# One normalisation instead of two, at both ends of a cross-attention over 8192 context rows

## The chip, the cores and the metric

The kernel runs on one core of a Trainium2 chip. The core has a matrix engine (PE, whose weight loads are listed apart as PEld), a vector engine (DVE), an activation engine (ACT), a general engine (POOL), a sync engine that issues transfers (SP), and 16 DMA engines. The metric is the device time of one execution in microseconds; lower is better.

## The reference, cut to what matters

A latent `x` of 512 rows by 512 columns passes through five blocks. Each block reads a row-normalised `x` and adds its output to `x`. The change touches the entry of the third-last block (cross-attention over 8192 context rows) and the entry of the second-last one (channel attention), because each of these two normalises its input once more:

```python
def _layernorm(x, axis=-1, eps=1e-05):
    m = jnp.mean(x, axis=axis, keepdims=True)
    v = jnp.var(x, axis=axis, keepdims=True)
    return (x - m) / jnp.sqrt(v + eps)
...
    # _L1_xattn_ref(x, latents, ...), EPS = 1e-05
    ln = layernorm(latents, gl, bl)      # (x - mu) * rsqrt(var + EPS) * g + b
    q = ln @ Wq
    kv_input = jnp.concatenate([xn, ln], axis=-2)
    kv = kv_input @ Wkv
...
    # _L1_attn_ref(x, gamma, ...), EPS = 1e-12
    xn = _l2norm(x) * dim ** 0.5 * gamma # t / max(sqrt(sum(t * t)), EPS)
    qkv = xn @ w_qkv
...
    x = x + _L1_xattn_ref(ctx_1024, _layernorm(x, axis=-1), L1_xattn_Wq, ...)
    x = x + _L1_attn_ref(_layernorm(x, axis=-1), L1_attn_gamma, ...)
    x = x + _L1_ffn_ref(_layernorm(x, axis=-1), ...)
```

So the rows are layer-normalised twice in a row ahead of the cross-attention, and layer-normalised and then scaled to unit length ahead of the channel attention.

## The kernel before

The 512 rows of `x` stay on the core in `x_res` as four tiles of 128 rows (index `tt`, `TT` = 4). Every engine has one program, written out by hand, and the engines meet through semaphores. There is no scheduler: the order of the calls is the order of the work.

A hand-over between two blocks is a short stretch of its own. The matrix engine ends the block with one output tile per `tt`. DVE adds the tile to `x_res` (line 1700 at the entry of the cross-attention, line 1869 at its exit, line 1953 at the exit of the channel attention). `ln_measure` (lines 1441 and 1442) takes mean and variance of the rows with two DVE instructions. POOL makes the scale from the variance with two small instructions: it adds the epsilon and raises to the power -0.5 (lines 813 and 814; at the cross-attention's entry lines 909 and 910 in `twice_scale`). `ln_row` (line 1447) writes the normalised tile `xn` on DVE. PE transposes the four tiles, and ACT and DVE split them into a high and a low half (`xT_hi`, `xT_lo`), with which the next block's products start. DVE handles tile `tt - 1` while POOL works on tile `tt`.

**Entry of the cross-attention.** After the first `ln_row` of a tile, DVE measures `xn` itself, POOL makes a second scale, and a second `ln_row` rescales `xn` in place. `TWICE` numbers the eight `ln_row` calls. PE transposes (line 2262) wait on the second one. Behind the last of them DVE inverts and splits the context's deviations (`sd`, lines 1711 to 1715), makes the low half of the query weights (`wq_lo`, line 1728), applies gain and bias (`affine`, line 1723) and splits the result (line 1743). PE meanwhile transposes `sd` (line 2267) and makes `bv` (line 2272: 32 products with one moving column each, whose stationary side is the raw weight `wkv_raw`); after them in its program come the query products (lines 2083 to 2085). The weights come by transfers that SP issues once the last output tile of the block before is complete:

```python
sp.wait_ge(s3_out, TT)
sp.dma_start(wq_raw[:], ...)     # line 662
sp.dma_start(wkv_raw[:], ...)    # line 663
```

ACT makes `wq_hi` from `wq_raw` (line 1195).

**Exit of the cross-attention.** After `ln_row`, ACT squares `xn` with a running sum (`sum_sq`, line 1300), POOL bounds the sum from below and raises it to -0.5 (lines 951 and 953), and DVE scales `xn` in place (`unit_row`, line 1864). PE transposes (line 2092) wait on that; then ACT and DVE split (lines 1304 and 1879), and the products of the channel attention start (line 2083).

Of the kernel before, what the change touches and what calls it, by code (L numbers as in the profile page):

```python
# [7 lines left out]
ACT = mybir.ActivationFunctionType  # L8
ALU = mybir.AluOpType
AX = mybir.AxisListType  # L10

P = 128
T = 512
D = 512
TT, DT = T // P, D // P
BANK = 512
LN_EPS = 1e-5
# [97 lines left out]

SQUARED = (1, 2, 4, 6)
UNIT_ROWS = [5 * TT + n for n in (3, 5, 7, 8)]
TWICE = ((0, 1, 3, 5), (2, 4, 6, 7))

# [79 lines left out]
def build(nc, a, out):  # L199
    ctx = ExitStack()  # L200
    with ctx:
# [186 lines left out]
        t5 = s5("t5", [P, XPAIRS])  # L388
        sum_sq = s5("sum_sq", [P, TT])

# [136 lines left out]
        def retire(engine, *counts):  # L527
# [13 lines left out]
        p5_mm, n5_sum, s5_sim, a5_T, o5_mm, s5_out = again("pe", "mm", "sum", "sim", "aT", "o", "out")  # L541
        w5_hi, x5_sq, p5_hi, p5_sq, t5_exp, s5_exp, a5_hi, o5_hi = again(
            "act", "w_hi", "x_sq", "p_hi", "p_sq", "t_exp", "exp", "a_hi", "o_hi")
        n5_sqrt = Signal(sem("n5_sqrt"))
        w5_lo, g5_ready, p5_lo, n5_read, s5_shift, s5_bd, a5_lo, o5_lo, s5_x = again(
            "dve", "w_lo", "gamma", "p_lo", "read", "shift", "bd", "a_lo", "o_lo", "x")
        x5_rn, n5_rs, bd_zero = again("pool", "rn", "rs", "zero")
        retire("pe", (p5_mm, UNITS), (n5_sum, 2 * XCB), (s5_sim, 2), (a5_T, 2), (o5_mm, XPAIRS), (s5_out, TT),
# [5 lines left out]
               (peak_neg, PAIRS), (shift_split, PAIRS), (o_inv, 1), (o_norm, PAIRS))  # L554
        retire("pool", (x5_rn, 2 * TT), (n5_rs, 1), (bd_zero, 1))
        retire("dma", (w4_q_loaded, 16), (w4_kv_loaded, 16), (w4_out_loaded, 16), (cT_loaded0, 16 * (KCHUNKS - 1) // 2), (cT_loaded1, 16 * (KCHUNKS - 1) // 2),
# [242 lines left out]
        def _(pool):  # L799
# [105 lines left out]

            def twice_scale(n, tt):

                pool.wait_ge(ln_stats, 3 * TT + n + 1)
                link(pool, nc.gpsimd.tensor_scalar(ln_ve[:, tt:tt + 1], ln_mv[:, tt, 1:2], LN_EPS, None, ALU.add))
                nc.gpsimd.tensor_tensor(ln_rstd[:, tt:tt + 1], ln_ve[:, tt:tt + 1], neg_half[:, tt:tt + 1], ALU.pow).then_inc(ln_scaled, 1)  # L910

            for n, tt in enumerate((0, 1, 0, 2, 1, 3, 2, 3)):
                twice_scale(n, tt)
            nc.gpsimd.memset(scale_rows[:].bitcast(F32), 0.0).then_inc(s4_init.sem, 1)
# [32 lines left out]
            def unit_scale(tt):  # L947

                one = slice(tt, tt + 1)
                pool.wait_ge(*x5_sq(tt + 1))  # L950
                nc.gpsimd.tensor_scalar(sum_sq[:, one], sum_sq[:, one], TINY, None, ALU.max).then_inc(x5_rn.sem, 1)
                pool.wait_ge(*x5_rn(2 * tt + 1))
                nc.gpsimd.tensor_tensor(sum_sq[:, one], sum_sq[:, one], neg_half[:, one], ALU.pow).then_inc(x5_rn.sem, 1)

            ln_scale(5, 0)
            for tt in range(1, TT):
                ln_scale(5, tt)
                unit_scale(tt - 1)
            unit_scale(TT - 1)
            nc.gpsimd.memset(attn_bd[:], 0.0).then_inc(bd_zero.sem, 1)  # L960
# [3 lines left out]

            ln_scales(6)
            link(pool, nc.gpsimd.memset(before[:], 1.0))
# [17 lines left out]
        def _(act_e):  # L984
# [312 lines left out]

            for tt in range(TT):
                act_e.wait_ge(xn_ready, 5 * TT + SQUARED[tt])
                nc.scalar.activation(squares[:, tt], xn[:, tt], ACT.Square, accum_out=sum_sq[:, tt:tt + 1]).then_inc(x5_sq.sem, 1)  # L1300
            act_e.wait_ge(*g5_ready(1))
# [3 lines left out]
            for c in range(3 * XCB):  # L1305
                for j in range(4):
# [13 lines left out]
                    if c < 2 * XCB:  # L1320
                        if j == 0:
                            if c == 0:
                                act_e.wait_ge(*x5_sq(TT))
                            else:
                                act_e.wait_ge(*n5_sum(c))
                        nc.scalar.activation(squares[:, j], ps[:, n % 4], ACT.Square).then_inc(p5_sq.sem, 1)
                        nc.scalar.activation(qk_hi[:, c // XCB, j, c % XCB * CB:(c % XCB + 1) * CB], ps[:, n % 4],
                                             ACT.Copy).then_inc(p5_hi.sem, 1)
                    else:
                        nc.scalar.activation(vT_hi[:, n - QK_UNITS], ps[:, n % 4], ACT.Copy).then_inc(p5_hi.sem, 1)  # L1330
# [45 lines left out]
            for tt in range(TT):  # L1376
                act_e.wait_ge(xn_ready, 7 * TT + tt + 1)
                if tt:
                    act_e.wait_ge(*x6_sq(tt))
                nc.scalar.activation(s_gate[:], xn[:, tt], ACT.Square, accum_out=r6[:, tt:tt + 1]).then_inc(x6_sq.sem, 1)  # L1380
# [55 lines left out]
        def _(dve):  # L1436
# [259 lines left out]
            level_out(HB // HQ - 1)  # L1696
            for tt in range(TT + 2):
                if tt < TT:
                    dve.wait_ge(s3_out, tt + 1)
                    nc.vector.scalar_tensor_tensor(x_res[:, tt], ps[:, tt], t_back[:, 1, tt:tt + 1], x_res[:, tt],  # L1700
                                                   ALU.mult, ALU.add).then_inc(s3_x, 1)
                    dve.wait_ge(s3_x, tt + 1)
                    ln_measure(tt, x_res)
                if 1 <= tt <= TT:
                    ln_row(3 * TT + TWICE[0][tt - 1], tt - 1, x_res)
                    dve.wait_ge(xn_ready, 3 * TT + TWICE[0][tt - 1] + 1)
                    ln_measure(tt - 1, xn)
                if tt >= 2:
                    ln_row(3 * TT + TWICE[1][tt - 2], tt - 2, xn)
            dve.wait_ge(rs_ready, 1)  # L1710
# [150 lines left out]

            def unit_row(tt):
                dve.wait_ge(*x5_rn(2 * tt + 2))
                nc.vector.tensor_scalar(xn[:, tt], xn[:, tt], sum_sq[:, tt:tt + 1], None, ALU.mult).then_inc(xn_ready, 1)

            for tt in range(TT + 2):
                if tt < TT:
                    dve.wait_ge(*s4_out(tt + 1))
                    nc.vector.tensor_tensor(x_res[:, tt], ps[:, 4 + tt], x_res[:, tt], ALU.add).then_inc(s4_x.sem, 1)
                    dve.wait_ge(*s4_x(tt + 1))  # L1870
                    ln_measure(tt, x_res)
                if 1 <= tt <= TT:
                    ln_row(5 * TT + tt - 1, tt - 1, x_res)
                if tt >= 2:
                    unit_row(tt - 2)
            dve.wait_ge(*g5_ready(1))
# [78 lines left out]

            ln_rows(6, add_fifth)
            ln_low(3)
# [121 lines left out]
        def _(pe):  # L2079
# [179 lines left out]
            for j in range(KT):  # L2259
                pe.wait_ge(xn_ready, 3 * TT + TWICE[1][j] + 1)  # L2260
                for dt in range(DT):
# [232 lines left out]

            ln_transpose(UNIT_ROWS)

# [80 lines left out]

            ln_transpose(range(7 * TT + 1, 8 * TT + 1))
            pe.wait_ge(xT_lo_ready, 4 * DT)
# [171 lines left out]
```

## Time and profile before

| | |
|---|---|
| time, three runs | 2758.85, 2763.52, 2764.38 us, median 2763.52 |
| profiled execution | 2763.65 us, its span 2761.9 us |
| PE busy | 2532.4 us, 92% of the span |
| DVE busy | 1852.6 us, 67% |
| ACT busy | 1109.3 us, 40% |
| POOL busy | 570.1 us, 21% |
| mean granted clock of PE | 0.957 |

Busy time is what an engine spent in instructions; a share of the span says nothing about which engine is waited for in a given stretch. In the rows further down, a timeline row is: start, duration, engine, line and operation, tile written and tiles read, shapes and count, and in brackets how long the engine had been idle and what released it.

### The profile page before, as it was taken

The page shows a single profiled execution, that of the slowest core. Times are in us where ns is not written, and L with a number is a line of the kernel's source. Part 1 is how long each engine was busy: PE and PEld are TensorE (multiplying, and loading weights), DVE is VectorE, ACT ScalarE, POOL GpSimd, SP SyncE. Part 2 cuts the span into 40 slices and gives each one's busy share as a digit, 9 for nine tenths or more (in the row PEclk, how much of TensorE's full clock was granted, in tenths as well). Part 3 has the DMA queues.
Part 4 walks back from the last instruction along what each step waited for, and adds up shares of the span by engine and source line. Part 5 has one row for each costly group of instructions (what it writes and reads, how often), then busy time and mean ns, then how long its engine had stood idle before and what let it go on. Part 6 is the DMA issues. An engine that isn't in the chain of part 4 may idle for free.

```text
span 2761.9 us, 33609 instructions
## 1 busy us (share of the span) xinstructions
PE 2532.4 (92%) x11618; PEld 1677.2 (61%) x11618; DVE 1852.6 (67%) x2025; ACT 1109.3 (40%) x1343; POOL 570.1 (21%) x413
## 2 busy tenths in 40 slices
PE   6999988967765799999999999999899799999999
PEld 5778867732222677777764444444477577777776
DVE  5877843189988677778886666666534666666665
ACT  2334322144435322222235555555332455554553
POOL 4555542078850211111110000000000100000000
PEclk9999989989986799999999999999989899999999
DMA  7677745710010233433322223222100366666663
GB/s 275 227 240 262 261 115 162 272 62 16 15 69 10 104 135 133 164 140 141 149 92 107 92 93 130 97 91 91 61 31 31 132 235 221 223 221 222 228 228 133
DMA packets 105455, 394.47 MB, mean 143 GB/s; under 512 B 22842, under 2 KB 23046, under 8 KB 73108
## 3 DMA queue, kind: packets, MB, share of 16 engines
q1 hardware_dynamic: 77380, 326.61, 32.3%
q10 hardware_dynamic: 27984, 66.66, 7.0%
q8 instruction: 56, 0.92, 0.1%
q14 instruction: 35, 0.29, 0.0%
HBM read 303.93 MB, written 89.30 MB: 142 GB/s over the span
## 4 chain that ended last, share of the span: by engine, by line
PE 77%; DVE 10%; DMA 6%; issue 3%; POOL 2%; ACT 1%; ACTq 0%; DVEq 0%; SPq 0%; POOLq 0%
PE ps L2083 17%; PE ps L2084 16%; PE ps L2085 16%; PE ps L2430 10%; PE ps L2439 9%; DVE ps L1595 4%; DMA w_halves<-unit_lo 4%; PE ps L2342 3%; DVE drive L1595 1%; PE ps L2673 1%; PE ps L2236 1%; POOL drive L878 1%; DMA sh_raw<-in_s_parts 1%; DMA wT_lo<-w_halves 1%; DVE ln_st L1441 1%
## 5 line engine op out<-in xcount | busy, mean ns | idle before, releaser
L1835 DVE TENSOR_TENSOR sums<-sums,pT 128x1024 f32<-128x1024 f32 x272 | 333.2, 1225 | 195.7 <-ACT pT L1270 181.4
L1778 DVE SCALAR_TENSOR_TENSOR peak<-ps,rs_all,peak 128x1024 f32<-128x1024 f32 x272 | 335.5, 1277 | 95.1 <-PE ps L2342 94.7
L1270 ACT ACTIVATE pT<-ps,rs_all 128x1024 f32<-128x1024 f32 x272 | 288.3, 1112 | 231.9 <-DVE sums L1835 128.5
L2439 PE MATMUL ps<-pT,values 128*64 128x512 f32 x1088 | 263.4, 605 | 0.0
L2188 PE MATMUL ps<-read,ident 128*128 128x512 f32 x256 | 144.7, 679 | 72.6 <-POOL read L891 37.2
L878 POOL TENSOR_TENSOR drive<-x_conv,bc_all 128x1024 f32<-128x1024 f32 x64 | 150.5, 2374 | 100.9 <-PE ps L2085 100.9
L926 POOL TENSOR_TENSOR cT_lo<-cT_raw,cT_hi 128x512 fp32r<-128x512 f32 x64 | 82.7, 1294 | 347.6 <-ACT cT_hi L1222 347.6
L1970 DVE TENSOR_TENSOR rgu_lo<-rgu_raw,rgu_hi 128x2048 fp32r<-128x2048 f32 x64 | 143.9, 2288 | 5.1 <-ACT rgu_hi L1353 5.1
L2188 PEld LDWEIGHTS ps<-read,ident 128*128 128x128 f32 x256 | 45.6, 205 | 166.7 <-DVE read L1601 77.4
L2439 PEld LDWEIGHTS ps<-pT,values 128*64 128x64 f32 x1088 | 66.0, 136 | 126.4 <-issue 126.4
L1136 ACT ACTIVATE ps<-delta,a_neg 128x512 f32<-128x512 f32 (+1 forms) x128 | 88.5, 692 | 126.8 <-DVE read L1601 113.4
L813 POOL TENSOR_SCALAR ln_ve<-ln_mv 128x1 f32<-128x1 f32 x20 | 7.3, 364 | 627.6 <-DVE ln_mv L1442 627.4
L826 POOL TENSOR_TENSOR ctx_lo<-ctx_raw,ctx_hi 128x512 fp32r<-128x512 f32 x64 | 106.2, 1660 | 129.4 <-DVE ctx_hi L1476 129.4
L1210 ACT ACTIVATE key_hi<-ps 128x512 fp32r<-128x512 f32 x68 | 40.7, 599 | 203.8 <-PE ps L2085 203.8
L2430 PE MATMUL ps<-q_lo,key_hi 64*128 64x512 f32 x544 | 121.2, 442 | 0.0
L2430 PEld LDWEIGHTS ps<-q_lo,key_hi 64*128 64x128 f32 x544 | 50.8, 183 | 115.5 <-ACT pT L1270 106.3
L1964 DVE TENSOR_TENSOR sh_lo<-sh_raw,sh_hi 128x1536 fp32r<-128x1536 f32 x32 | 56.3, 1758 | 93.2 <-ACT sh_hi L1348 93.2
L1353 ACT ACTIVATE rgu_hi<-rgu_raw 128x2048 fp32r<-128x2048 f32 x64 | 118.8, 1907 | 0.0
L1595 DVE TENSOR_TENSOR_SCAN ps<-ps,drive 128x512 f32<-128x512 f32 x96 | 116.9, 1218 | 2.2 <-POOL drive L878 2.2
L2083 PE MATMUL ps<-xT_hi,ctxT_lo 128*128 128x512 f32 x256 | 102.8, 402 | 14.4 <-DVE ctxT_lo L1478 14.4
L2083 PE MATMUL ps<-cT_hi,wp_lo 128*128 128x512 f32 x256 | 107.8, 421 | 8.9 <-POOL cT_lo L926 8.9
L1215 ACT ACTIVATE values<-ps,rs_all 128x512 f32<-128x512 f32 x68 | 46.9, 690 | 163.5 <-PE ps L2085 163.5
(436 smaller groups left out, 6362.3 us busy)
## 6 DMA issues: line engine op xcount, KB each, us to landing
rgu_raw<-in_r_gate_up SPq DMA_DIRECT2D x64, 1024.0 KB, 4.8
rd_raw<-in_r_down SPq DMA_DIRECT2D x32, 1024.0 KB, 4.8
sh_raw<-in_s_parts SPq DMA_DIRECT2D x32, 768.0 KB, 4.3
key_rows<-key_hi SPq DMA_DIRECT2D x17, 1024.0 KB, 3.9
key_rows<-key_lo SPq DMA_DIRECT2D x17, 1024.0 KB, 5.9
value_rows<-values SPq DMA_DIRECT2D x17, 1024.0 KB, 8.7
ctxT_raw<-in_ctx_T SPq DMA_DIRECT2D x16, 1024.0 KB, 6.7
ctx_raw<-in_ctx SPq DMA_DIRECT2D x16, 1024.0 KB, 8.6
```

The source lines that it names most:

```text
L878: nc.gpsimd.tensor_tensor(drive[:, g % SCAN_AHEAD], x_conv[:, ib].unsqueeze(1).to_broadcast([P, SG, T]), b_all[:, g * SG:(g + 1) * SG], AL ...
L1270: nc.scalar.activation(pT[:, kt], ps[:, kt % 2 * 2:kt % 2 * 2 + 2], ACT.Exp, scale=rs_all[:, bass.ds(c * KT + kt, 1)]).then_inc(s4_exp.sem, 1)
L1595: nc.vector.tensor_tensor_scan(source if far(g, e) else ps[:, DECAY_BANK + e], ps[:, DECAY_BANK + e], source, 0.0, ALU.mult, ALU.add).then ...
L1778: nc.vector.scalar_tensor_tensor(peak[:, p], ps[:, b:b + 2], rs_all[:, bass.ds(c * KT + kt, 1)], peak[:, p], ALU.mult, ALU.max).then_inc(s ...
L1835: nc.vector.tensor_tensor(sums[:, p], sums[:, p], pT[:, kt], ALU.add).then_inc(s4_sum.sem, 1)
L1970: nc.vector.tensor_tensor(rgu_lo[:, j % 2, i], rgu_raw[:, j % 2, i], rgu_hi[:, j % 2, i].bitcast(F32), ALU.subtract).then_inc(rgu_low.sem, 1)
L2083: nc.tensor.matmul(o, l_lo, r_hi, start=start, stop=False)
L2084: nc.tensor.matmul(o, l_hi, r_lo, start=False, stop=False)
L2085: return nc.tensor.matmul(o, l_hi, r_hi, start=False, stop=stop)
L2188: done = nc.tensor.matmul(ps[:, b], ident[:], read[:, g % SCAN_AHEAD, e], start=g == 0 and e == 0, stop=g == SGS - 1 and e == SG - 1)
L2430: done = nc.tensor.matmul(ps[:, kt % 2 * 2 + e], key[rows], query[rows], start=m == 0, stop=m == len(parts) - 1)
L2439: done = nc.tensor.matmul(ps[e * DK:(e + 1) * DK, 4 + p], values[:, s, kt, h * DK:(h + 1) * DK], pT[:, kt, e], start=start and kt == 0, st ...
```

## The change

Both double normalisations become one. With v the variance of a row and e the epsilon, the second layer normalisation sees variance v / (v + e), so both scales together are (v(1 + e) + e²)^-0.5. At the exit the sum of squares of the normalised row is D v / (v + e), so both scales together are (D v)^-0.5, bounded as before. In each case POOL computes the product directly from the first variance, in the same two instructions with other constants, and `ln_row` runs once for a tile. The second measuring, the four ACT squares, the tile `sum_sq`, the second POOL pair and the second DVE scaling are gone. The numbers for which `xn_ready`, `ln_stats` and `ln_scaled` are waited follow.

```diff
-SQUARED = (1, 2, 4, 6)
-UNIT_ROWS = [5 * TT + n for n in (3, 5, 7, 8)]
-TWICE = ((0, 1, 3, 5), (2, 4, 6, 7))
...
-            def twice_scale(n, tt):
-
-                pool.wait_ge(ln_stats, 3 * TT + n + 1)
-                link(pool, nc.gpsimd.tensor_scalar(ln_ve[:, tt:tt + 1], ln_mv[:, tt, 1:2], LN_EPS, None, ALU.add))
+            def twice_scale(tt):
+
+                pool.wait_ge(ln_stats, 3 * TT + tt + 1)
+                link(pool, nc.gpsimd.tensor_scalar(ln_ve[:, tt:tt + 1], ln_mv[:, tt, 1:2], 1.0 + LN_EPS, LN_EPS * LN_EPS, ALU.mult, ALU.add))
...
-            for n, tt in enumerate((0, 1, 0, 2, 1, 3, 2, 3)):
-                twice_scale(n, tt)
+            for tt in range(TT):
+                twice_scale(tt)
...
-                one = slice(tt, tt + 1)
-                pool.wait_ge(*x5_sq(tt + 1))
-                nc.gpsimd.tensor_scalar(sum_sq[:, one], sum_sq[:, one], TINY, None, ALU.max).then_inc(x5_rn.sem, 1)
-                pool.wait_ge(*x5_rn(2 * tt + 1))
-                nc.gpsimd.tensor_tensor(sum_sq[:, one], sum_sq[:, one], neg_half[:, one], ALU.pow).then_inc(x5_rn.sem, 1)
-
-            ln_scale(5, 0)
-            for tt in range(1, TT):
-                ln_scale(5, tt)
-                unit_scale(tt - 1)
-            unit_scale(TT - 1)
+                pool.wait_ge(ln_stats, 4 * TT + tt + 1)
+                link(pool, nc.gpsimd.tensor_scalar(ln_ve[:, tt:tt + 1], ln_mv[:, tt, 1:2], float(D), TINY * LN_EPS, ALU.mult, ALU.max))
+                nc.gpsimd.tensor_tensor(ln_rstd[:, tt:tt + 1], ln_ve[:, tt:tt + 1], neg_half[:, tt:tt + 1], ALU.pow).then_inc(ln_scaled, 1)
+
+            for tt in range(TT):
+                unit_scale(tt)
...
-            for tt in range(TT):
-                act_e.wait_ge(xn_ready, 5 * TT + SQUARED[tt])
-                nc.scalar.activation(squares[:, tt], xn[:, tt], ACT.Square, accum_out=sum_sq[:, tt:tt + 1]).then_inc(x5_sq.sem, 1)
...
-            for tt in range(TT + 2):
+            for tt in range(TT + 1):
...
-                if 1 <= tt <= TT:
-                    ln_row(3 * TT + TWICE[0][tt - 1], tt - 1, x_res)
-                    dve.wait_ge(xn_ready, 3 * TT + TWICE[0][tt - 1] + 1)
-                    ln_measure(tt - 1, xn)
-                if tt >= 2:
-                    ln_row(3 * TT + TWICE[1][tt - 2], tt - 2, xn)
+                if tt:
+                    ln_row(3 * TT + tt - 1, tt - 1, x_res)
...
-                if 1 <= tt <= TT:
-                    ln_row(5 * TT + tt - 1, tt - 1, x_res)
-                if tt >= 2:
-                    unit_row(tt - 2)
+                if tt:
+                    ln_row(4 * TT + tt - 1, tt - 1, x_res)
...
-                pe.wait_ge(xn_ready, 3 * TT + TWICE[1][j] + 1)
+                pe.wait_ge(xn_ready, 3 * TT + j + 1)
...
-            ln_transpose(UNIT_ROWS)
+            ln_transpose(range(4 * TT + 1, 5 * TT + 1))
```

This is DVE's program at the entry of the cross-attention before the change, the end of the eight normalisations and what stands behind them (`xn` are the normalised rows, `ln_mv` mean and variance, `sd` the context's deviations):

```order
L1441 BN_STATS ln_st<-xn 128x6
L1442 BN_AGGR ln_mv<-ln_st 128x2
L1447 TENSOR_SCALAR xn<-xn,ln_mv,ln_rstd 128x512
L1447 TENSOR_SCALAR xn<-x_res,ln_mv,ln_rstd 128x512
L1441 BN_STATS ln_st<-xn 128x6
L1442 BN_AGGR ln_mv<-ln_st 128x2
L1447 TENSOR_SCALAR xn<-xn,ln_mv,ln_rstd 128x512 x2
L1711 RECIPROCAL sd<-rs_all 128x68
```

The same place after the change, from the last addition to `x_res` on:

```order
L1686 SCALAR_TENSOR_TENSOR x_res<-ps,t_back,x_res 128x512
L1427 BN_STATS ln_st<-x_res 128x6
L1428 BN_AGGR ln_mv<-ln_st 128x2
L1433 TENSOR_SCALAR xn<-x_res,ln_mv,ln_rstd 128x512 x2
L1693 RECIPROCAL sd<-rs_all 128x68
L1694 CAST sd_parts<-sd 128x68
```

The twelve DVE instructions that read `xn` are gone, and the inversion of `sd` stands directly behind the fourth normalisation; nothing else moved.

This is DVE's program at the exit of the cross-attention before the change (`sum_sq` is the sum of squares of a row, `gamma` the gain):

```order
L1869 TENSOR_TENSOR x_res<-ps,x_res 128x512
L1441 BN_STATS ln_st<-x_res 128x6
L1442 BN_AGGR ln_mv<-ln_st 128x2
L1447 TENSOR_SCALAR xn<-x_res,ln_mv,ln_rstd 128x512
L1864 TENSOR_SCALAR xn<-xn,sum_sq 128x512
L1447 TENSOR_SCALAR xn<-x_res,ln_mv,ln_rstd 128x512
L1864 TENSOR_SCALAR xn<-xn,sum_sq 128x512 x2
L1879 SCALAR_TENSOR_TENSOR xT_lo<-ps,gamma_52,xT_hi 128x512 x4
```

And after it:

```order
L1847 TENSOR_TENSOR x_res<-ps,x_res 128x512
L1427 BN_STATS ln_st<-x_res 128x6
L1428 BN_AGGR ln_mv<-ln_st 128x2
L1433 TENSOR_SCALAR xn<-x_res,ln_mv,ln_rstd 128x512 x2
L1855 SCALAR_TENSOR_TENSOR xT_lo<-ps,gamma_52,xT_hi 128x512 x4
```

The four scalings by `sum_sq` are gone from DVE, and each addition to `x_res` follows the normalisation directly.

Besides, the semaphores are dealt out again, since two are no longer needed. In the loop over six experts of the last block, DVE's program has 5 register instructions more in a turn, which compute the values that it waits for; the programs of PE and SP have the same rows as before.

## Rows read from the trace of the kernel before

**Rows 1.** Windows: busy time by stretch, clock and DMA share.

```profile
core 0: us, PE busy (x) PEld busy (x) DVE busy (x) ACT busy (x) POOL busy (x), PEclk, DMA share, GB/s
891.00:915.00 24.00, 14.49 (x64) 11.11 (x62) 22.23 (x41) 6.34 (x7) 8.58 (x17) 0.61 0.59 223
968.00:1975.00 1007.00, 1003.92 (x5408) 590.73 (x5408) 714.39 (x626) 407.19 (x467) 84.36 (x66) 1.00 0.29 114
1996.00:2011.00 15.00, 6.75 (x26) 4.52 (x25) 11.51 (x22) 4.98 (x12) 8.22 (x17) 0.70 0.10 38
```

**Rows 2.** Timeline of DVE, entry of the cross-attention.

```profile
891.35 0.75 DVE L1700 SCALAR_TENSOR_TENSOR x_res<-ps,t_back,x_res 128x512 f32<-128x512 f32 x1 [2.41 <-PE ps L2246]
892.97 0.72 DVE L1700 SCALAR_TENSOR_TENSOR x_res<-ps,t_back,x_res 128x512 f32<-128x512 f32 x1
...
905.41 1.14 DVE L1447 TENSOR_SCALAR xn<-xn,ln_mv,ln_rstd 128x512 f32<-128x512 f32 x1 [0.77 <-POOL ln_rstd L910]
...
907.63 2.29 DVE L1728 TENSOR_TENSOR wq_lo<-wq_raw,wq_hi 128x2048 fp32r<-128x2048 f32 x1
912.72 2.48 DVE L1743 TENSOR_TENSOR xT_lo<-affine,xT_hi 128x512 fp32r<-128x512 f32 x4
```

**Rows 3.** Timeline of SP, ACT and PE, the same place.

```profile
894.37 0.51 SPq L663 DMA_DIRECT2D wkv_raw<-in_L_xattn_Wkv  x1
899.40 1.91 ACT L1195 ACTIVATE wq_hi<-wq_raw 128x2048 fp32r<-128x2048 f32 x1 [11.18 <-DMA wq_raw<-in_L_xattn_Wq]
907.80 6.95 PEld L2272 LDWEIGHTS ps<-b_ctx,wkv_raw 128*128 128x128 f32 x32
915.26 0.79 PE L2083 MATMUL ps<-xT_hi,wq_lo 128*128 128x512 f32 x1 [0.42 <-DVE xT_lo L1743]
```

**Rows 4.** Tile wkv_raw: its one transfer from issue to landing.

```profile
DMA to landing us min/median/max: 10.2/10.2/10.2
```

**Rows 5.** Timeline of DVE, exit of the channel attention.

```profile
2140.99 0.69 DVE L1953 TENSOR_TENSOR x_res<-ps,x_res 128x512 f32<-128x512 f32 x1 [7.52 <-PE ps L2085]
...
2142.55 0.66 DVE L1953 TENSOR_TENSOR x_res<-ps,x_res 128x512 f32<-128x512 f32 x1
...
2149.30 0.55 DVE L1447 TENSOR_SCALAR xn<-x_res,ln_mv,ln_rstd 128x512 f32<-128x512 f32 x1 [0.77 <-POOL ln_rstd L814]
```

**Rows 6.** Timeline, exit of the cross-attention.

```profile
1995.88 0.69 DVE L1869 TENSOR_TENSOR x_res<-ps,x_res 128x512 f32<-128x512 f32 x1 [3.33 <-PE ps L2085]
...
2004.83 0.55 DVE L1447 TENSOR_SCALAR xn<-x_res,ln_mv,ln_rstd 128x512 f32<-128x512 f32 x1 [0.46 <-POOL ln_rstd L814]
...
2007.13 1.14 DVE L1864 TENSOR_SCALAR xn<-xn,sum_sq 128x512 f32<-128x512 f32 x1 [0.81 <-POOL sum_sq L953]
...
2010.60 0.76 PE L2083 MATMUL ps<-w_hi,xT_lo 128*128 128x512 f32 x1 [1.15 <-DVE xT_lo L1879]
```

**Rows 7.** Windows of 1 us where the clock of PE rises.

```profile
920.00:921.00 1.00, 1.00 (x5) 0.78 (x5) 0.00 (x0) 0.47 (x1) 1.00 (x2) 0.98 0.00 0
...
2015.00:2016.00 1.00, 1.00 (x4) 0.85 (x3) 0.00 (x0) 0.00 (x1) 0.00 (x0) 0.64 0.00 0
```

**Rows 8.** Chain that ended last: products after a restart, at either clock.

```profile
1985.22 0.76 PE ps L2083
...
1988.11 0.43 PE ps L2083
1989.00 0.24 PE ps L2083
```

**Rows 9.** Timeline of DVE, two steps of the expert loop, two written out.

```profile
2320.64 0.68 DVE L2059 TENSOR_TENSOR r_act<-ps,r_gate 80x512 f32<-80x512 f32 x1
2337.43 0.68 DVE L2059 TENSOR_TENSOR r_act<-ps,r_gate 80x512 f32<-80x512 f32 x1
...
2655.97 0.68 DVE L2059 TENSOR_TENSOR r_act<-ps,r_gate 80x512 f32<-80x512 f32 x1
2672.68 0.68 DVE L2059 TENSOR_TENSOR r_act<-ps,r_gate 80x512 f32<-80x512 f32 x1
```

More of the change, by code:

```diff
@@ L388, in build @@
         t5 = s5("t5", [P, XPAIRS])
-        sum_sq = s5("sum_sq", [P, TT])
         s6 = Map(nc, base, 229344)
@@ L541, in build @@
         p5_mm, n5_sum, s5_sim, a5_T, o5_mm, s5_out = again("pe", "mm", "sum", "sim", "aT", "o", "out")
-        w5_hi, x5_sq, p5_hi, p5_sq, t5_exp, s5_exp, a5_hi, o5_hi = again(
-            "act", "w_hi", "x_sq", "p_hi", "p_sq", "t_exp", "exp", "a_hi", "o_hi")
+        w5_hi, p5_hi, p5_sq, t5_exp, s5_exp, a5_hi, o5_hi = again(
+            "act", "w_hi", "p_hi", "p_sq", "t_exp", "exp", "a_hi", "o_hi")
         n5_sqrt = Signal(sem("n5_sqrt"))
@@ L546, in build @@
             "dve", "w_lo", "gamma", "p_lo", "read", "shift", "bd", "a_lo", "o_lo", "x")
-        x5_rn, n5_rs, bd_zero = again("pool", "rn", "rs", "zero")
+        n5_rs, bd_zero = again("pool", "rs", "zero")
         retire("pe", (p5_mm, UNITS), (n5_sum, 2 * XCB), (s5_sim, 2), (a5_T, 2), (o5_mm, XPAIRS), (s5_out, TT),
@@ L554, in build @@
                (peak_neg, PAIRS), (shift_split, PAIRS), (o_inv, 1), (o_norm, PAIRS))
-        retire("pool", (x5_rn, 2 * TT), (n5_rs, 1), (bd_zero, 1))
+        retire("pool", (n5_rs, 1), (bd_zero, 1))
         retire("dma", (w4_q_loaded, 16), (w4_kv_loaded, 16), (w4_out_loaded, 16), (cT_loaded0, 16 * (KCHUNKS - 1) // 2), (cT_loaded1, 16 * (KCHUNKS - 1) // 2),
@@ L962, in _ @@
             nc.gpsimd.tensor_tensor(rq[:], rq[:], neg_half[:, 0:XPAIRS], ALU.pow).then_inc(n5_rs.sem, 1)
-            ln_scales(6)
+            ln_scales(5)
             link(pool, nc.gpsimd.memset(before[:], 1.0))
@@ L1321, in _ @@
                         if j == 0:
-                            if c == 0:
-                                act_e.wait_ge(*x5_sq(TT))
-                            else:
+                            if c:
                                 act_e.wait_ge(*n5_sum(c))
@@ L1376, in _ @@
             for tt in range(TT):
-                act_e.wait_ge(xn_ready, 7 * TT + tt + 1)
+                act_e.wait_ge(xn_ready, 5 * TT + tt + 1)
                 if tt:
@@ L1860, in _ @@
             qkv_lo(1)
[L1862 to L1866, printed above, removed]
+            for tt in range(TT + 1):
                 if tt < TT:
@@ L1954, in add_fifth @@
                 dve.wait_ge(*s5_x(tt + 1))
-            ln_rows(6, add_fifth)
+            ln_rows(5, add_fifth)
             ln_low(3)
@@ L2575, in _ @@
                     weigh_rows(p + 4)
-            ln_transpose(range(7 * TT + 1, 8 * TT + 1))
+            ln_transpose(range(5 * TT + 1, 6 * TT + 1))
             pe.wait_ge(xT_lo_ready, 4 * DT)
```

## The prediction

> **What bounds the kernel now.** I read the busy time by stretch first, since the change touches two short stretches only. In the long middle of the cross-attention PE is busy in 1003.9 of 1007 us: that part is PE's own, and a change ahead of it can only shift it. The two hand-overs are the opposite. Around the entry PE has work for 14.5 of 24 us, around the exit for 6.8 of 15 us, and DVE for 22.2 and 11.5 us [rows 1]. The reader is to see that in a hand-over the normalisation itself is the path: what it gets shorter by is time gained, until something else is last.
>
> The timelines tell what is last. At the entry DVE goes from the first addition at 891.35 to the start of the eighth row normalisation at 905.41, then on to the weights' low half at 907.63 and to the last split, which ends at 912.72 + 2.48 = 915.20 [rows 2]. The first query product starts at 915.26, and PE had been idle for only 0.42 us before it [rows 3]. This is the point of the whole case: two chains arrive there almost together. DVE's arrives at 915.20. PE's own arrives at 915.26 - 0.42 = 914.84, with the 32 `bv` products that began at 907.80. Shortening DVE's chain alone would be worth 0.4 us; more comes only if PE's chain moves as well.
>
> At the exit there is one chain: first addition at 1995.88, last scaling at 2007.13, first product at 2010.60 with PE waiting for DVE's split [rows 6].
>
> **The change, part by part.** It removes work and adds none. For the new length of a hand-over I don't add up single instructions, because DVE and POOL interlock; the kernel has a hand-over of exactly the new form at the exit of the channel attention: four additions, four measurings, four row normalisations, two POOL instructions for each. There it is 2149.30 - 2140.99 = 8.31 us from the first addition to the start of the last normalisation [rows 5].
>
> *Entry, DVE.* The addition is the three-operand form here, and one step takes 892.97 - 891.35 = 1.62 us where the other place takes 1.56 [rows 2, 5]. Four such steps add 0.24, so 8.55 us: the last normalisation starts at 899.9 instead of 905.41, 5.5 us earlier. I let it keep its 1.14 us, since POOL's instruction behind the last scale, which is a memset at both ends here, still comes beside it. Everything that DVE does next comes 5.5 us earlier, if nothing else stops it. `wq_lo` would start at 902.1; its other input is ready at 899.40 + 1.91 = 901.3 [rows 3], so it isn't stopped, with 0.8 us to spare. The last split ends at 909.7.
>
> *Entry, PE.* The transposes of `xn` and `sd` move with DVE, so the `bv` products could start at 907.80 - 5.5 = 902.3. They read `wkv_raw`. SP issued this load at 894.37, released by the end of the block before and not by any normalisation, so it doesn't move; it took 10.2 us to land [rows 3, 4], which is 904.6. In the kernel before this is hidden by 3.2 us. Now it is what PE waits for: `bv` starts at 904.6. From its first weight load to the point where PE was free took 914.84 - 907.80 = 7.04 us, so PE is free at 911.6, after DVE's 909.7. The first query product starts at 911.6 instead of 915.26: a gain of 3.6 us out of DVE's 5.5. What is late next is thus a transfer and the row of one-column products behind it.
>
> Its bounds: if the load landed only just before 907.80, which the trace doesn't exclude by any wait of PE, the entry gives 0.4; if it doesn't hold PE at all, DVE's 5.5 count in full.
>
> The Trainium skill (DMA: Bandwidth & Descriptors, section on the anatomy of one DMA) gives about 2.0 us plus bytes at 436 GB/s for a transfer, with a fit made on another issuing path than SP's. As an estimate for this load with the 1 MB of `wq_raw` ahead of its own 2 MB that is 9.2 us, a landing at 903.6, a first product at 910.6, and a gain of 7.6 for the whole change (2755.9). The trace has this very transfer with 10.2 us, so the sum goes by the trace.
>
> *Exit.* 1995.88 + 8.31 = 2004.19 for the start of the last normalisation; before, the last scaling started at 2007.13 [rows 5, 6]. All that follows (transposes, splits, first product) hangs on it alone, since the weights' halves are made before 1995.88. Gain 2.9 us. From below: the round behind the last row normalisation (square, two POOL instructions, scaling) is gone in any case, which is 2007.13 - 2004.83 = 2.3. From above: if the last normalisation took 0.55 as in rows 5 and not 1.14 as the one that it replaces, 3.5.
>
> *The work taken from ACT and POOL* has no price of its own: four squares and sixteen small POOL instructions lay inside the chains already counted. The wait on the squares ahead of the first products is a wait on something long done.
>
> *Register instructions.* Five more on DVE in each of six turns of the expert loop. A loop step takes 2337.43 - 2320.64 = 16.79 us, the same step written out without any register work 2672.68 - 2655.97 = 16.71 [rows 9]. So all register work of all engines in a step costs 0.08, and even its doubling in 24 steps would be 1.9 us. DVE has the slack in a step to cover five more; I take 0.
>
> *Clock.* After each of these breaks PE's products start at the lower clock, 1.2 GHz, and rise after some time: at the entry 915.26 to about 920.0, at the exit 2010.60 to 2015.7 (a clock of 0.64 as the mean of that microsecond), and elsewhere 1985.22 to about 1988.4 [rows 3, 6, 7, 8]. The breaks stay longer than 9 us, so PE starts at the lower clock again. But the slow stretch can be 3.2 to 5.1 us long, and a product takes 0.43 there against 0.23 or 0.24 behind it, so one microsecond of it costs 0.47. If both stretches came out at the shortest instead of the present 4.7 and 5.1, that is 1.6 us less; I allow as much the other way, and 0 in the sum.
>
> Sum: 3.6 + 2.9 = 6.5 us. Against the profiled execution's own 2763.65 us that gives 2757.1; that execution lies 0.1 above the median of the runs shown, so the median goes from 2763.5 to 2757.0. Behind each of the two points I expect only a shift: PE sets the pace of the cross-attention's middle, and every load there is released by work that moves along.
>
> **The rivals.**
>
> *The load holds PE longer.* For: the landing is given once, from one execution, and the first reader came 3.2 us behind it, so a landing up to 907.8 would look the same to PE. Against: 10.2 us is a direct figure. Then the entry gives 0.4 and the exit 2.9: 3.3 us, 2760.2.
>
> *The load doesn't hold PE.* For: the transfer may be quicker in other executions, and the margin in question is 904.6 against 902.3. Against: the same figure. Then 5.5 + 2.9 = 8.4 us, 2755.1.
>
> *The shift is given back.* A point further on is set by something that keeps its time, as the load does here: the context chunks are issued right behind it. For: that is the mechanism just found. Against: PE's 1003.9 busy of 1007 us leave no room where a fixed time could hide. Then near 2763.5.
>
> *Slower.* PE now waits about 2 us for a load between transposes and `bv`, and this pause could delay the rise of its clock in the cross-attention's first products. The price is 0.20 us for each product that stays low. It takes (6.5 + 5.5) / 0.20 = 60 products more at the lower clock to end at 2769, over 0.2% slower; all 144 products of the first latent block would be 2783. Against: in three restarts, with different work ahead of each, the clock was up within 5.1 us.
>
> **How the numbers follow.** 0.2% of this kernel is 5.5 us, about what a measurement of it can tell from no change. The forecast of 6.5 us has 0.62; since it lies only 1.0 above that line and the clock alone scatters by 1.6, I count 0.50 of it as faster and 0.12 as within 0.2%. The load holding longer has 0.15 (within), not holding 0.15 (faster), given back 0.04 (within), slower 0.04 with everything unforeseen. Faster 0.65, same 0.31, slower 0.04. The range goes from the second rival with the clock in its favour, 2755.1 - 1.6 = 2753.5, to the first with most of it against, 2760.2 + 1.3 = 2761.5; the last two cases and some tail are left out.
>
> **What would show it.** In the changed kernel's trace, 8.5 us from the first addition to the last normalisation at the entry and 8.3 at the exit. PE idle ahead of the `bv` products, put down to the transfer of `wkv_raw`; then the first query product right behind the last of the 32, with DVE's split done some 2 us before. From the block's last output tile to the first query product 3.6 us less than now, and 2.9 less at the exit. The long middle as long as before to within a microsecond, and the expert step at 16.8. The prediction is wrong if `bv` starts without a wait at some 902.3, if the split is still what PE waits for, or if the middle of the cross-attention gets longer by what the entry gained.

## The result, and the profile after

| | before | after |
|---|---|---|
| median | 2759.9 us (20 runs, the three shown among them; 2752.65 to 2765.07) | 2753.49 us (20 runs; 2748.69 to 2757.20) |
| span of the profiled execution | 2761.9 us | 2751.0 us |
| granted clock, mean | 0.957 | 0.962 |

The ratio of after to before is 0.9974, with a 95% interval of 0.9967 to 0.9981: lower by 0.26%, some 7.2 us, and 6.4 us between the two medians. The interval leaves out 1, but its end lies just short of the 0.2% line (0.998) that the prediction draws. The forecast was 6.5 us and a time of 2757.0 (2753.5 to 2761.5). The change did what was forecast; the time lies 3.5 us below the forecast and 0.01 us below the range.

The page of the changed kernel, part 1, has 4.7 us less of DVE's busy time, 10.1 less of POOL's and 3.0 less of ACT's, none of which by itself says anything on the time. The difference isn't the work taken out either: the sixteen DVE instructions that are gone held 8.8 us in the trace of before, and two groups of splits far from the change (`ctxT_lo` and `unit_lo`) take 3.8 us more in this one.

```profile
PE 2528.7 (92%) x11615; PEld 1675.0 (61%) x11618; DVE 1847.9 (67%) x2009; ACT 1106.3 (40%) x1335; POOL 560.0 (20%) x397
```

The entry of the cross-attention after the change, timeline of DVE (columns as in [rows 2]). The first addition is at 888.37, so the last normalisation stands at +8.50 where the forecast had +8.55.

```profile
888.37 0.75 DVE L1686 SCALAR_TENSOR_TENSOR x_res<-ps,t_back,x_res 128x512 f32<-128x512 f32 x1 [1.60 <-PE ps L2222]
...
896.87 1.14 DVE L1433 TENSOR_SCALAR xn<-x_res,ln_mv,ln_rstd 128x512 f32<-128x512 f32 x1 [0.71 <-POOL ln_rstd L906]
...
899.09 2.29 DVE L1710 TENSOR_TENSOR wq_lo<-wq_raw,wq_hi 128x2048 fp32r<-128x2048 f32 x1
...
904.18 2.49 DVE L1725 TENSOR_TENSOR xT_lo<-affine,xT_hi 128x512 fp32r<-128x512 f32 x4
```

The same place on PE. It answers to [rows 3]: the bracket on the 32 `bv` products says 1.96 us of idle time ended by the transfer of `wkv_raw`, where before there was no bracket at all, and the first query product has no bracket now.

```profile
901.64 6.99 PE L2248 MATMUL ps<-b_ctx,wkv_raw 128*128 128x1 f32 x32 [1.96 <-DMA wkv_raw<-in_L_xattn_Wkv]
908.49 0.77 PE L2059 MATMUL ps<-xT_hi,wq_lo 128*128 128x512 f32 x1
```

The chain that ended last says the same in four lines (start, us, what): the issue at 891.39, 10.21 us of transfer, the one-column products, the query products.

```profile
891.39 10.21 DMA wkv_raw<-in_L_xattn_Wkv
901.59 0.04 issue
901.64 6.99 PE ps L2248 x32
908.63 0.64 PE ps L2059
```

The exit, DVE's and PE's timelines, to be held against [rows 6]: first addition, last normalisation at +8.30 (forecast +8.31), first product at +11.76.

```profile
1988.40 0.69 DVE L1847 TENSOR_TENSOR x_res<-ps,x_res 128x512 f32<-128x512 f32 x1 [3.49 <-PE ps L2061]
...
1996.70 1.14 DVE L1433 TENSOR_SCALAR xn<-x_res,ln_mv,ln_rstd 128x512 f32<-128x512 f32 x1 [0.76 <-POOL ln_rstd L947]
...
2000.16 0.77 PE L2059 MATMUL ps<-w_hi,xT_lo 128*128 128x512 f32 x1 [1.15 <-DVE xT_lo L1855]
```

And the long middle, the window that answers to the second row of [rows 1]: PE is busy in 1003.84 of 1007 us, as before.

```profile
961.00:1968.00 1007.00, 1003.84 (x5408) 590.72 (x5408) 714.89 (x626) 406.78 (x467) 84.25 (x66) 1.00 0.29 114
```

From here on one cut serves for every kernel. The span is taken apart at four rows: the first addition of the entry, the first query product, the first addition of the exit, the first product behind it. *Entry* and *exit* are the two hand-overs; *ahead*, *middle* and *behind* are the rest. All in us, each from one profiled execution:

| | ahead | entry | middle | exit | behind | span |
|---|---|---|---|---|---|---|
| before | 891.35 | 23.91 | 1080.62 | 14.72 | 751.3 | 2761.9 |
| after | 888.37 | 20.12 | 1079.91 | 11.76 | 750.8 | 2751.0 |
| difference | 2.98 | 3.79 | 0.71 | 2.96 | 0.5 | 10.9 |

The two stretches that the change touches give 6.75 us. The other 4.2 us of this pair of profiles lie where both kernels do the same work.

### The profile page after: what moved, and what is told of

The parts are those of the page before. It is cut to its first block, busy times and chain, and to the rows that moved or that the text cites. A ratio compares the mean times of both kernels' runs of the same rounds, so it can differ in the third digit from the quotient of the medians.

```text
span 2751.0 us, 33583 instructions
## 1 busy us (share of the span) xinstructions
PE 2528.7 (92%) x11615; PEld 1675.0 (61%) x11618; DVE 1847.9 (67%) x2009; ACT 1106.3 (40%) x1335; POOL 560.0 (20%) x397
## 4 chain that ended last, share of the span: by engine, by line
PE 78%; DVE 10%; DMA 6%; issue 3%; POOL 1%; ACT 1%; ACTq 0%; DVEq 0%; SPq 0%; POOLq 0%
PE ps L2059 17%; PE ps L2060 16%; PE ps L2061 16%; PE ps L2406 10%; PE ps L2415 9%; DMA w_halves<-unit_lo 4%; DVE ps L1581 4%; PE ps L2318 3%; DVE drive L1581 1%; PE ps L2649 1%; PE ps L2212 1%; DMA wT_lo<-w_halves 1%; PE ps L2222 1%; DMA x_res<-in_x 1%; POOL drive L874 1%
## 5 line engine op out<-in xcount | busy, mean ns | idle before, releaser
L946 POOL TENSOR_SCALAR ln_ve<-ln_mv 128x1 f32<-128x1 f32 x4 | 1.5, 385 | 545.1 <-DVE ln_mv L1428 545.1
```

## The experiments

### One end alone

The entry's half and the exit's half of the diff, each as a kernel.

Entry only, against the kernel before:

```diff
-            for n, tt in enumerate((0, 1, 0, 2, 1, 3, 2, 3)):
-                twice_scale(n, tt)
+            for tt in range(TT):
+                twice_scale(tt)
```

Exit only:

```diff
-            ln_scale(5, 0)
-            for tt in range(1, TT):
-                ln_scale(5, tt)
-                unit_scale(tt - 1)
-            unit_scale(TT - 1)
+            for tt in range(TT):
+                unit_scale(tt)
```

> The kernel before with the single normalisation at the entry of the cross-attention only. Theory (the weights' load caps the gain): the entry, from the first addition to the first query product, takes 20.1 us as in the changed kernel instead of 23.9, the exit stays at 14.7, and the time falls by 3.8 us, ratio 0.9986. Rival (the whole gain comes from the exit, the entry is covered): ratio 1.000 and an entry of 23.9. Rival (the two edits need each other): anything else than 3.8.

> The changed kernel with the entry of the cross-attention as before, so the single normalisation at the exit only. Theory: exit 11.8 us instead of 14.7, entry 23.9, time lower by 3.0 us, ratio 0.9989. With the entry's 3.8 us the two parts add up to the whole, 6.8. Rival (given back in the channel attention): exit shorter, but the stretch from its first product to the end longer than the 751 us of both traces.

| | ahead | entry | middle | exit | behind | median, ratio to before in the same set of runs |
|---|---|---|---|---|---|---|
| entry only | 889.44 | 20.08 | 1080.07 | 14.73 | 753.7 | 2763.21, 1.0005 [0.9993, 1.0017] |
| exit only | 888.60 | 23.92 | 1080.39 | 11.76 | 750.8 | 2759.12, 0.9988 [0.9978, 0.9997] |

Each half changes its own stretch by what it gives in the whole (3.83 and 2.96) and leaves the other alone to 0.01 us: the two gains are independent and add up. The exit alone also shows in the time (2.96 of 2761 would be 0.9989). The entry alone doesn't: 3.8 us would be 0.9986, which lies outside its interval. Its profile can't say why the median is so high, since that execution took 2759.75 us, 3.5 below the median of its own kernel. It does show how a stretch that no edit reaches can differ, near its end, among the last expert's products. In the kernel before, the clock is at 1.00 in each of the last 5 us windows from 2740 to 2755; here it falls in the second and is back early in the third (the clock is the third value from the right):

```profile
2740.00:2745.00 5.00, 3.81 (x19) 2.19 (x17) 0.69 (x1) 0.22 (x1) 0.00 (x0) 1.00 0.00 0
2745.00:2750.00 5.00, 4.11 (x12) 2.39 (x12) 0.49 (x1) 0.22 (x1) 0.00 (x0) 0.69 0.00 0
2750.00:2755.00 5.00, 4.12 (x10) 1.44 (x8) 2.23 (x4) 0.59 (x1) 0.00 (x0) 0.97 0.19 74
```

From the second last expert's output to the last one's it takes 56.41 us, and 54.71 in the kernel before. So a stretch that both share differs by 1.7 us.

### The whole change and the entry alone, once more

The same two kernels in other runs, to separate a cause from chance. No edit.

> The changed kernel once more, as the yardstick for the other three and as a second draw of its profile. Theory (each hand-over is a fixed chain, the rest of the time scatters with PE's clock): entry 20.1 us, exit 11.8 us to within 0.1, ratio to before 0.9974 to within 0.001, while the stretches between differ by up to 3 us from the first profile. Rival (the gain found was partly luck of one set of runs): ratio 0.999 or above.

> The entry-only kernel once more, because its time came out at 1.0005 of before although its entry was 3.8 us shorter. Theory (scatter of the clock in the last block): entry 20.1 again, ratio 0.9986, the stretch behind the exit back at some 751 us. Rival (this build is slower somewhere else by 4 to 5 us each time): ratio 1.0005 again and the last block at 753 to 754 us again.

| | ahead | entry | middle | exit | behind | median, ratio |
|---|---|---|---|---|---|---|
| whole | 896.73 | 20.01 | 1080.66 | 11.77 | 751.1 | 2756.0, 0.9973 [0.9963, 0.9984] |
| entry only | 886.14 | 19.94 | 1080.09 | 14.72 | 750.8 | 2760.93, 0.9992 [0.9980, 1.0003] |

The whole change repeats its ratio to 0.0001. The entry's second interval holds 0.9986, and both of its intervals hold 1. *Behind* is back at 750.8, so the rival of a build that is slower there each time fell; why the first set came out at 1.0005 stays open. Entry and exit repeat to 0.14 us, but *ahead* differs by 8.4 us between two executions of the same program (888.37 and 896.73), where I had expected up to 3. Nothing of the change stands there. The scatter of one execution is thus larger than what the entry gives, and the time of these 11 and 12 runs doesn't show it; the stretch does.

### The load is what PE waits for

The rivals of the entry's 3.6 us were about `wkv_raw`. Three edits move its landing. First, its half for the values, the one that `bv` reads, comes ahead of the rest:

```diff
-            sp.dma_start(wkv_raw[:], ...).then_inc(w4_loaded[1].sem, 16)
+            sp.dma_start(wkv_raw[:, :, D:2 * D], wkv_cols[:, :, D:2 * D]).then_inc(w4_loaded[1].sem, 16)
+            sp.dma_start(wkv_raw[:, :, 0:D], wkv_cols[:, :, 0:D]).then_inc(w4_rest, 16)
```

ACT waits for both halves before it makes `wkv_hi` from them.

Second, one chunk of the context is loaded ahead of it, so that it lands later:

```diff
+            load_chunk(chunks[0], 1)
             sp.dma_start(wkv_raw[:], ...).then_inc(w4_loaded[1].sem, 16)
-            load_chunk(chunks[0], 1)
             load_chunk(chunks[1], 0)
```

> The changed kernel, but the load of wkv_raw is split in two, and the half that the one-column products read goes first. Theory (PE waits for this load): the half lands some 2.5 us earlier, the products start as soon as the transposes are done at 10.7 to 11.3 us from the first addition instead of 13.3, PE is free at about 18.3 and the split is done at 18.3: the entry takes 18.3 to 18.4 us instead of 20.1, time 1.8 us lower than the changed kernel, ratio to before 0.9968. Rival (the wait shown is not what sets the end, DVE's chain is): entry stays at 20.1.

> The changed kernel with one of the two 1 MB context chunks issued ahead of wkv_raw, which delays its landing by 1 MB of transfer, some 2.6 us. Theory: PE waits 2.6 us longer, 4.6 instead of 2.0, and the entry takes 22.7 us, time 2.6 us above the changed kernel, ratio to before about 0.9984. Rival (DVE's chain sets the end): entry 20.1, no change.

PE's rows at the entry, values first:

```profile
903.45 6.95 PE L2252 MATMUL ps<-b_ctx,wkv_raw 128*128 128x1 f32 x32
910.70 0.79 PE L2063 MATMUL ps<-xT_hi,wq_lo 128*128 128x512 f32 x1 [0.29 <-DVE xT_lo L1729]
```

And with a chunk ahead:

```profile
905.81 6.99 PE L2248 MATMUL ps<-b_ctx,wkv_raw 128*128 128x1 f32 x32 [4.48 <-DMA wkv_raw<-in_L_xattn_Wkv]
```

| | `bv` starts after the first addition | entry | middle | time, ratio |
|---|---|---|---|---|
| after | 13.27 (waits 1.96) | 20.12 | 1079.91 | above |
| values first | 11.10 (no wait) | 18.35 | 1081.93 | 2757.26, 0.9981 [0.9967, 0.9995] |
| chunk ahead | 15.79 (waits 4.48) | 22.64 | 1080.72 | 2760.48, 0.9995 [0.9983, 1.0007] |

The bracket goes away in the one and grows by 2.52 in the other, and the entry follows by 2.52. With the load out of the way the entry takes 18.35 us, which is 5.56 less than before: DVE's 5.5 in full. The next in line is then DVE's split again, by 0.29 us, and the load is barely out of the way: its first half lands at +11.02, and `bv` starts at +11.10. Both sides of the forecast's limit are shown by the stretches. The times don't show them: I had expected 0.9968 and 0.9984, and 0.9981 and 0.9995 came out, with intervals that just hold the forecasts. Values first doesn't come out below the change's 0.9974 either. Its middle is 2.0 us longer than the change's, which takes back the 1.8 us that its entry is shorter; the last section comes back to that.

The same edit on the kernel before says where the load landed there, which that trace could not say by any wait. The chunks' own calls, which stood behind the load, move ahead of it:

```diff
 # on the kernel before, one or both chunks
+            load_chunk(chunks[0], 1)
+            load_chunk(chunks[1], 0)
             sp.dma_start(wkv_raw[:], ...).then_inc(w4_loaded[1].sem, 16)
```

> The kernel before with one 1 MB context chunk issued ahead of wkv_raw. Theory: its landing moves by 2.6 us, from 13.3 to 15.9 us behind the first addition, and the one-column products start at 16.5 there, so nothing waits: entry 23.9 us as before. In the changed kernel the same edit made the entry 2.5 us longer. Rival (the load was already at the limit before): entry above 24.2.

> The kernel before with both context chunks, 2 MB, issued ahead of wkv_raw. Theory: landing at about 18.4 us behind the first addition, 1.9 us after the one-column products want to start; PE is free at 18.4 + 7.0 = 25.4 and DVE's split is long done: entry 25.4 to 25.5 us instead of 23.9. Rival (something else hides it): 23.9.

The kernel before has this row, at +16.66 and without a bracket:

```profile
908.01 6.83 PE L2272 MATMUL ps<-b_ctx,wkv_raw 128*128 128x1 f32 x32
```

With one chunk ahead `bv` starts at +16.66 as well, without a wait, and the entry takes 23.91. With both PE waits:

```profile
912.43 6.99 PE L2272 MATMUL ps<-b_ctx,wkv_raw 128*128 128x1 f32 x32 [1.25 <-DMA wkv_raw<-in_L_xattn_Wkv]
```

That is +18.12 from the first addition at 894.31, and an entry of 24.96, half a us less than I had expected. Two chunks put the landing 18.12 - 13.27 = 4.85 us later, 2.4 each, so in the kernel before it lay at about +13.3, and with one chunk at +15.8, still ahead of the +16.66 at which PE asked for it. The landings that the traces give for the transfer itself say the same: +13.25, +15.66 and +18.07. (Single runs of 2765.17 and 2768.39 us stand for these two, beside 2762.73 for before.)

### The 1.14 us of the last normalisation

The forecast kept 1.14 us for it because POOL's memset comes beside it at both ends. After the change these are POOL's two rows, for normalisations that start at 896.87 and 1996.70:

```profile
896.78 0.95 POOL L910 MEMSET scale_rows<- 128x1024 f32 x1
...
1996.62 0.95 POOL L951 MEMSET attn_bd<- 128x1024 f32 x1
```

Here both memsets are moved behind later work of POOL:

```diff
-            nc.gpsimd.memset(scale_rows[:].bitcast(F32), 0.0).then_inc(s4_init.sem, 1)
...
+            nc.gpsimd.memset(scale_rows[:].bitcast(F32), 0.0).then_inc(s4_init.sem, 1)
             pool.wait_ge(*w4_hi(2 + DT))
...
-            nc.gpsimd.memset(attn_bd[:], 0.0).then_inc(bd_zero.sem, 1)
...
             nc.gpsimd.tensor_tensor(rq[:], rq[:], neg_half[:, 0:XPAIRS], ALU.pow).then_inc(n5_rs.sem, 1)
+            nc.gpsimd.memset(attn_bd[:], 0.0).then_inc(bd_zero.sem, 1)
```

> The changed kernel with POOL's two memsets that run beside the last row normalisation (scale_rows at the entry, attn_bd at the exit) put behind later POOL work. Theory: the normalisation takes 0.5 us instead of 1.14 at both places; the exit gets 0.6 us shorter, 11.2 us, since DVE's chain sets its end; the entry stays at 20.1, since PE waits there for the load. Rival (DVE's chain sets both): entry 19.5 as well. The time falls by 0.6 or 1.2 us, less than the timing can tell.

> The changed kernel with both additions: the values' half of the load first, and the memsets later. Theory: with the load out of the way DVE's chain sets the end of the entry, and now its 0.6 us count there too: entry 17.7 us, exit 11.2 us, in sum 3.0 us less than the changed kernel, ratio to before 0.9963. Rival (the half load itself is then last): entry 18.3.

> The kernel with both additions once more, since only few of its runs were undisturbed. Theory: entry 17.8 and exit 11.2 us again, 6.1 and 3.5 us less than before, in sum 9.6 us, ratio to before 0.9965. Rival (this build gains more elsewhere as well): 0.9951 again.

DVE's last normalisation, entry and exit, memsets moved:

```profile
902.12 0.55 DVE L1433 TENSOR_SCALAR xn<-x_res,ln_mv,ln_rstd 128x512 f32<-128x512 f32 x1 [0.72 <-POOL ln_rstd L906]
...
2002.61 0.55 DVE L1433 TENSOR_SCALAR xn<-x_res,ln_mv,ln_rstd 128x512 f32<-128x512 f32 x1 [0.76 <-POOL ln_rstd L947]
```

| | entry | middle | exit | behind | median, ratio |
|---|---|---|---|---|---|
| memsets later | 20.13 | 1080.56 | 11.17 | 757.6 | 2758.96, 0.9985 [0.9973, 0.9997] |
| memsets later, values first | 17.81 | 1082.77 | 11.17 | 755.5 | 2749.77, 0.9951 [0.9935, 0.9968] |
| the same, once more | 17.77 | 1082.48 | 11.17 | 757.7 | 2754.64, 0.9967 [0.9953, 0.9980] |

Both went from 1.14 to 0.55 us, so the memset beside them was the cause. At the exit that is worth its 0.59 us (11.76 to 11.17), the upper bound of 3.5 in the forecast. At the entry it is worth nothing by itself, since PE waits for the load (now 2.55 us instead of 1.96), and 0.5 to 0.6 more once the values' half comes first (18.35 to 17.8). There PE again waits for the load in two of three profiles, 0.18 and 0.21 us, and the first query product follows the one-column products without a wait: the load and the row of products behind it are last once more.

But *behind* is 4 to 7 us longer in all three than in the changed kernel. To tell the two memsets apart, the last kernel has values first and only the entry's memset moved:

> The changed kernel with the load of the values' half of the weights first, and with the memset of the context's scale rows moved behind the low half of the latents; the memset of the block diagonal at the exit stays where the change has it. So it is the pair of edits of the run before without its exit half. In the three profiles with both memsets moved, the stretch from the first exit product to the end took 755.5 to 757.7 us, against 750.4 to 751.3 in most others. Theory A (the exit's memset, put behind the scale of the queries, costs that): here the stretch from the first squares of the channel attention to its first transposed values is 58.1 us as in the change, not 61.3, and the stretch behind the exit is within 750 to 752. Theory B (the clock of the matrix engine, by chance or by what the entry does): 61.3 or something between, although the exit is unchanged. Under both the entry takes 17.8 us and the exit 11.76 with 1.14 us for the last normalisation. Time: 2763.0 less 6.1 at the entry and 3.0 at the exit gives about 2754 at the level of the runs of before; it is 0.997 of before.

It has an entry of 17.77, a middle of 1082.18, an exit of 11.77 and 751.4 *behind*; 2752.65 us, 0.9963 [0.9951, 0.9976]. From the first squares of the channel attention to its first transposed values it takes 58.1 us, as every kernel with the exit's memset in place (58.06 to 58.17 in eleven profiles); the three with that memset moved take 61.3 to 61.4. So 3.2 us of the longer *behind* go with the memset; the rest is of the size by which *behind* differs among the others. The place is seen in the clock. After the change, windows of 4 us behind the exit:

```profile
2037.00:2041.00 4.00, 4.00 (x22) 3.39 (x22) 0.69 (x1) 1.48 (x3) 0.00 (x0) 1.00 0.00 0
2041.00:2045.00 4.00, 4.00 (x20) 3.30 (x19) 2.09 (x2) 3.47 (x5) 0.00 (x0) 1.00 0.00 0
```

And with the memsets moved, the same work, 5.5 us later as the first squares are (2010.97 and 2005.47):

```profile
2042.50:2046.50 4.00, 4.00 (x15) 3.52 (x16) 0.69 (x1) 1.09 (x2) 0.00 (x0) 0.50 0.00 0
2046.50:2050.50 4.00, 4.00 (x14) 3.21 (x13) 0.04 (x1) 1.16 (x3) 0.00 (x0) 0.71 0.00 0
```

PE is busy all of the time in both, and at 1.2 instead of 2.4 GHz behind one of the rows of one-column products that make the sums of squares. So moving this memset wins 0.6 us and loses 3.2. That the loss goes with this memset is shown by three profiles with it moved and eleven without; why the clock falls there is not, since PE has no idle time in those 58 to 61 us, neither in the change nor in the three.

## Why the time missed the range, and the change did not

**The entry, 3.6 us.** Right in mechanism and size: 3.79 measured, 3.8 to 4.0 in four profiles of it. Last normalisation at +8.50 (forecast 8.55); landing 10.21 us behind the issue (10.2); `bv` at +13.27 (904.6 - 891.35 = 13.25); DVE's split done at 904.18 + 2.49, which is +18.30 (18.35); first query product at +20.12 (911.6 - 891.35 = 20.25). The rest of 0.13 is in the forecast's 7.04. It counts from the first weight load at 907.80, which ran ahead while PE was still at its transposes; the products themselves began at 908.01, so the row took 6.83 us before and 6.85 after. The fit of the Trainium skill (DMA: Bandwidth & Descriptors, section on the anatomy of one DMA) would have had it land 1.0 us sooner; this transfer took 10.21 us again, so the trace's own figure was the right one to take. With a landing 1.0 sooner the whole gain would have been 7.6.

**The exit, 2.9 us.** Right: 2.96, and an exit of 11.76 or 11.77 in each of the six profiles that have this half with its memset in place. The chain of one exit could be read off another exit of the same form, [rows 5], to 0.01 us.

**The rivals.** "The load holds PE longer" fell: the landing is at +13.3, measured by PE's wait after the change and worked out from the two chunks for the kernel before, and not at +16.6. "The load doesn't hold PE" fell, and came true once the load was split. "The shift is given back" fell for this change: the middle took 1079.9 to 1080.7 with it, 1080.6 without. It came true for the faster entry, below. "Slower, by the clock" fell: of the first products behind the entry 10 took the 0.63 us or more of the lower clock where 11 had before, and behind the exit 11 as before. So the 0 that the sum had for the clock at these two places held.

**Register instructions, 0.** Right as far as it can be seen: a step of the expert loop takes 2326.48 - 2309.69 = 16.79 us after, as in [rows 9].

```profile
2309.69 0.68 DVE L2035 TENSOR_TENSOR r_act<-ps,r_gate 80x512 f32<-80x512 f32 x1
2326.48 0.68 DVE L2035 TENSOR_TENSOR r_act<-ps,r_gate 80x512 f32<-80x512 f32 x1
```

**The step that failed** is this one: "that execution lies 0.1 above the median of the runs shown, so the median goes from 2763.5 to 2757.0". It takes the median of three runs as the level of the kernel. Those three spread over 5.5 us, and 20 runs of the same kernel spread over 12.4 with a median of 2759.9, 3.6 lower. The gain of 6.5 was right to 0.1 against the two medians, and 2759.9 less 6.5 is 2753.4. So close a match is partly luck, since the ratio makes it 7.2 us and its interval allows 5.2 to 9.1; it is also luck on which side of the range's end a time falls that is 0.01 us beyond it. That the centre was 3.5 us too high is the level's 3.6. In the later sets of runs the kernel before had medians of 2760.95, 2762.45, 2762.73 and 2763.32, and the changed kernel one of 2756.0, which the range holds. So the level itself moves by 3.4 us between sets (each of the four later ones ran on a chip of its own, so chip and set can't be told apart), and the range had no term for that: its ends were those of two rivals with 1.6 and 1.3 us of clock. That I put the clock's scatter at 1.6 from the two restarts next to the change was the same mistake. Stretches far from the change scatter too: *ahead* differs by 8.4 us between two profiles of one program, and the last expert by 1.7 between two kernels that share it. In the last expert the clock is seen to fall. In *ahead* not all of it is the clock: the second profile is 1.6 us late at 110 us and 3.6 at 310, and from 100 to 350 us both have a clock of 1.00. What makes that part is open.

**What the difference of the profiles was worth.** The spans differ by 10.9 us, the medians by 6.4, and the two stretches by 6.75. Who takes the gain from one pair of spans is 4 us off, and the table of stretches says where: in *ahead*, *middle* and *behind*.

**A better version?** Values first and the entry's memset moved give 0.9963 [0.9951, 0.9976] against 0.9974 [0.9967, 0.9981] of the change: its entry is 2.3 us shorter, but the intervals overlap, so a gain on top isn't shown. The stretches speak against one: entry and middle together take 1099.95 us in it, 1100.28 with the values first alone, and 1100.03 and 1100.67 in the two profiles of the change. With both memsets moved the two sets gave 0.9951 and 0.9967, whose intervals overlap these too.

## What to carry to other kernels

In a short hand-over, write down for each engine when it would be free if it waited for nothing; a chain that is shortened gains only down to the next of these, and a load that is hidden today by 3 us is the wait of tomorrow. Ordering that load by its first use takes the wait away, as it did here (`bv` 2.2 us earlier); look whether the gain is still there at the end of the stretch behind it, since here it wasn't. And give the level a term of its own in the range: cut the span at fixed rows to read what the change did, and take from the spread of repeated runs how far the time can lie from it.

## What was unexpected of the hardware

**A gain at the entry came back as clock, twice.** All four profiles with the values first, and so the shortest entries (17.8 to 18.4 us), have a middle of 1081.9 to 1082.8. All others have 1079.9 to 1080.7, but for the kernel before with both chunks ahead, whose entry is the longest and whose middle is 1082.4. Of the 2.0 us between the change and values first, 0.7 were first won up to the context's first product, and 1.26 and 1.43 then lost at two restarts of PE: from the first row below to the last 1969.56 - 960.99 = 1008.57 against 1972.36 - 962.53 = 1009.83, and from there to the exit's first addition 18.84 against 20.27. The first restart is at the context's first product, behind 8.88 us of idle time in both kernels. After the change, from that product on, in windows of 5 us:

```profile
960.99:965.99 5.00, 5.00 (x18) 3.74 (x18) 0.00 (x0) 0.55 (x2) 0.00 (x0) 0.70 0.69 236
965.99:970.99 5.00, 5.00 (x26) 3.71 (x24) 4.27 (x4) 1.26 (x3) 1.30 (x1) 1.00 0.02 5
```

The same with the values first:

```profile
962.53:967.53 5.00, 5.00 (x12) 3.82 (x12) 0.00 (x0) 0.00 (x0) 0.00 (x0) 0.50 0.70 236
967.53:972.53 5.00, 5.00 (x23) 3.55 (x22) 3.43 (x4) 1.51 (x3) 1.29 (x1) 0.93 0.02 5
```

The idle time and the work are the same, but 18 products against 12 are done in the first 5 us. The second restart is at the end of the attention, where eight products take 5.84 us in the one and 7.19 in the other behind the same idle time of 3.54:

```profile
1969.56 5.84 PE L2459 MATMUL ps<-row_inv,head_rows 8*128 8x512 f32 x8 [3.54 <-DVE row_inv L1826]
```

```profile
1972.36 7.19 PE L2463 MATMUL ps<-row_inv,head_rows 8*128 8x512 f32 x8 [3.54 <-DVE row_inv L1830]
```

What the clock did at these restarts is thus not told by the length of the pause and the work behind it alone; the only difference between the two programs lies at the entry, some 50 us ahead of the first of them. That the longer middle came in all four profiles speaks for a cause and not for chance, but no run here singles it out; a short entry alone isn't it, as the kernel with both chunks ahead shows.

**A memset on POOL doubles a normalisation on DVE that runs beside it**, 1.14 against 0.55 us for the same 128x512 tile, at both ends. Moving only the entry's memset brought only the entry's normalisation to 0.55.
